# The late router gates as powers of e on GpSimd, one Gelu table load, and a new order in the last rounds of a decoder layer

## The reference, cut to what matters

```python
x = layernorm(x + linear_attention(x))              # softmax over q's head dim and over k's tokens
x = layernorm(x + cross_attention(x, ctx, ctx))     # 16 heads of 16
g = gelu(xt @ wg1 + bg1); logits = g @ wg2          # the router, 8 experts
probs = softmax(logits); top_vals, top_idx = top_k(probs, 2)
h = gelu(xt @ w_in[e]); o = h @ w_out[e]            # every expert, hidden size 512
y = sum over the two chosen experts of top_val * o
x = layernorm(x + y)
```

## Time and profile before

| | us |
|---|---|
| median of 3 executions | 430.15 |
| lowest, highest | 430.11, 433.90 |
| the profiled execution | 431.93 |
| its span, first to last instruction | 430.10 |

### The profile page before, as it was taken

How to read it: one execution, slowest core, us unless ns; L and a number is a source line. 1 busy time by engine, 2 the same in 40 slices (tenths; PEclk the granted TensorE clock), 3 DMA queues, 4 the chain that set the end, 5 groups by cost and what they waited for, 6 DMA issues and landing times. The chain is left out here.

```text
span 430.1 us, 12345 instructions
## 1 busy us (share of the span) xinstructions
PE 347.9 (81%) x4025; PEld 281.0 (65%) x4025; DVE 308.3 (72%) x912; ACT 222.1 (52%) x518; POOL 220.7 (51%) x287
## 2 busy tenths in 40 slices
PE   2977999999999999999887185759999999999200
PEld 1655777777777877777664053547899999988100
DVE  3767899888988889888777077468677666755193
ACT  3435676667666676766763045353544444444034
POOL 8335456676666766667258554643133333422273
PEclk9999999999999999999898588569999999999855
DMA  7520022220122211221012222325525322321393
GB/s 219 179 76 27 2 75 75 75 77 21 56 75 77 75 39 38 76 75 50 2 53 100 87 77 79 109 76 151 156 81 155 84 69 61 98 75 39 124 378 122
DMA packets 21387, 38.35 MB, mean 89 GB/s; under 512 B 3696, under 2 KB 11120, under 8 KB 21328
## 3 DMA queue, kind: packets, MB, share of 16 engines
q1 hardware_dynamic: 16768, 26.06, 19.8%
q0 software_dynamic: 3408, 9.41, 6.1%
q10 hardware_dynamic: 1152, 2.10, 1.3%
HBM read 24.71 MB, written 12.84 MB: 87 GB/s over the span
## 5 line engine op out<-in xcount | busy, mean ns | idle before, releaser
L575 POOL DMA_INDIRECT parts<-QKT,rows_all x39 | 37.8, 969 | 76.1 <-DVE QKT L1207 65.9
L328 PE MATMUL bank<-QS,EW 128*128 128x256 f16 (+1 forms) x384 | 62.6, 265 | 5.6 <-DVE XB L1021 5.6
L491 POOL TENSOR_TENSOR rstd<-veps,neghalf 128x1 f32<-128x1 f32 x48 | 39.6, 824 | 41.6 <-DVE veps L844 41.2
L1382 PE MATMUL bank<-EW,QV 128*128 x312 | 48.7, 273 | 1.8 <-DVE R L1199 0.8
L328 PE MATMUL bank<-XB,EW 128*128 128x256 f16 (+1 forms) x192 | 49.0, 264 | 0.0
L1199 DVE TENSOR_TENSOR R<-scratch,QV 128x512 f16<-128x512 f32 x39 | 26.7, 691 | 29.4 <-ACT scratch L764 17.9
L1126 DVE TENSOR_REDUCE NM<-bank 128x4 bf16<-128x512 f32 x64 | 39.6, 678 | 11.1 <-remote 10.1
L328 PEld LDWEIGHTS bank<-QS,EW 128*128 x384 | 37.7, 102 | 11.6 <-issue 6.1
L764 ACT ACTIVATE scratch<-bank 128x512 f32<-128x512 f32 x39 | 23.4, 600 | 40.5 <-PE bank L328 38.5
L506 POOL DMA_INDIRECT bkt<-REC,dest x32 | 32.9, 1029 | 21.3 <-issue 11.9
L699 ACT ACTIVATE rows_all<-bank 128x512 f32<-128x512 f32 x64 | 33.2, 603 | 18.2 <-remote 10.8
(11 more groups left out here) (240 smaller groups left out, 941.4 us busy)
## 6 DMA issues: line engine op xcount, KB each, us to landing
scratch<-w_in SPq DMA_DIRECT2D x8, 512.0 KB, 3.3
scratch<-w_out SPq DMA_DIRECT2D x8, 512.0 KB, 3.8
rows_all<-bkt SPq DMA_DIRECT2D x15, 262.0 KB
XC<-x SPq DMA_DIRECT2D x16, 128.0 KB, 3.3
XC<-ctx SPq DMA_DIRECT2D x16, 128.0 KB, 3.2
EW<-parts SPq DMA_DIRECT2D x8, 256.0 KB, 6.8
EW<-parts ACTq DMA_DIRECT2D x8, 256.0 KB, 7.4
out<-rows_all SPq DMA_DIRECT2D x8, 256.0 KB, 2.1
```

The costliest lines, as they stand in the source:

```text
L328: last = pe.matmul(dst, a(c), b(c), start=(c == 0 and i == 0), stop=(c == n - 1 and i == 2))
L491: pool.tensor_tensor(rstd[n][p][:], veps[n][p][:], neghalf[:, 0:1], ALU.pow).then_inc(s_rs[n], 1)
L575: pool.indirect_dma_start(parts, bass.IndirectOffsetOnAxis(ap=home[:, t, f:f + 1], axis=0), Y[t % 2][:, f, :], None).then_inc(s_put[t % 2] ...
L1382: last = pe.matmul(bank[4 + t % 2][:, f * D:(f + 1) * D], a[t % 2][:, h, f * P:(f + 1) * P], b[:, h, :], start=(h == 0 and i == 0 and f == 0),
```

## The change

Two things. The exponentials of groups 1 and 2 leave ScalarE: GpSimd computes them as powers of a constant tile `euler`, and ScalarE loads the Gelu table once, at a new step `hot:0` after the last reciprocal (group 0's exponentials stay on ScalarE). And the tails of GpSimd, VectorE and TensorE have a new order; on TensorE the up product of tile 0 is cut into two halves, `upa` and `upb`.

```diff
+        euler = sb("euler", [P, 1])
...
+            pool.memset(euler[:], float(np.exp(1.0))).then_inc(s_cst, 1)
...
+                if step == "exps":
+                    pool.wait_ge(s_off, b + 1)
+                    rows = slice(EDGE[b], EDGE[b + 1])
+                    n = EDGE[b + 1] - EDGE[b]
+                    pool.tensor_tensor(LE[:, rows, :].rearrange("p b e -> p (b e)"), euler[:].to_broadcast([P, n * NE]),
+                                       L[:, rows, :].rearrange("p b e -> p (b e)"), ALU.pow).then_inc(s_le, 1)
+                if step == "second":
+                    pool.wait_ge(s_gap, b + 1)
...
+                    pool.tensor_tensor(second[:, rows], euler[:].to_broadcast([P, EDGE[b + 1] - EDGE[b]]), gap[:, rows], ALU.pow)\
+                        .then_inc(s_second, 1)
...
-                     "lns:15 rec:15 X2T:13 gcp:13 gelu:1 X2T:14 exps:1 X2T:15 second:1 gcp:15 gelu:2 high:0 "
-                     "exps:2 second:2 high:1")
-            act.preload_act_table(ACT.Gelu)
+                     "lns:15 rec:15 hot:0 X2T:13 gcp:13 gelu:1 X2T:14 X2T:15 gcp:15 gelu:2 high:0 high:1")
...
-                     "x2T:13 cntpre:1 gh:13 ao2:15 x2T:14 lg:1 x2T:15 gh:15 cnt:1 lg:2 turn:0 cntpre:2 up:0 turn:1 cnt:2")
+                     "x2T:13 cntpre:1 gh:13 ao2:15 x2T:14 lg:1 x2T:15 gh:15 turn:0 cnt:1 cntpre:2 lg:2 upa:0 cnt:2 turn:1 upb:0")
```

More of the change, by code:

```diff
@@ L451, in _ @@
                 pool.memset(V2[p][:], 0.0).then_inc(s_cst, 1)
-            pool.wait_ge(s_cst, 11)
+            pool.wait_ge(s_cst, 12)
             for t in (ident, identb):
@@ L480, in _ @@
             pool.iota(spare_i[:], [[TW, MAXT], [P, HALVES]], base=0, channel_multiplier=1).then_inc(s_cst, 1)
-            pool.wait_ge(s_cst, 18)
+            pool.wait_ge(s_cst, 19)
             pool.affine_select(out=before[:], in_=before[:], compare_op=ALU.is_ge, fill=0.0, base=-1,
@@ L564, in _ @@
                      "pw0:14 qn:15 n1:14 x1b:14 n2:11 nr:12 pw0:15 "
[3 rows of a table removed]
+                     "pw1:15 sc:0 sc:1 sc:2 sc:3 x1b:15 sc:4 sc:5 pw2:12 sc:6 sc:7 sc:8 sc:9 sc:10 sc:11 pw2:13 sc:12 sc:13 sc:14 sc:15 sc:16 "
+                     "pw2:14 sc:17 sc:18 sc:19 pw2:15 "
+                     "exps:1 second:1 sc:20 sc:21 sc:22 sc:23 sc:24 sc:25 exps:2 second:2 sc:26 sc:27 sc:28 sc:29 sc:30 sc:31")
             def put(t):
@@ L710, in emit @@
                     gate_hidden(EDGE[b], EDGE[b + 1])
+                if step == "hot":
+                    act.preload_act_table(ACT.Gelu)
                 if step == "back":
@@ L1184, in _ @@
                      "QM1:14 R1:15 s1:15 "
[L1185 to L1188, removed]
+                     "mx0:14 n1:15 mx1:14 mx2:14 mx3:14 R2:12 s2:12 O2T:13 nr:13 QM1:15 full:0 n2:12 mx0:15 mx1:15 mx2:15 "
+                     "mx3:15 R2:13 s2:13 full:1 O2T:14 nr:14 full:2 n2:13 ewl:15 ewl:16 R2:14 s2:14 ewl:17 O2T:15 nr:15 R2:15 s2:15 n2:14 "
+                     "choice1:1 n2:15 choice2:1 gate1:1 dest:1 gate2:1 low:0 "
+                     "choice1:2 choice2:2 gate1:2 dest:2 gate2:2 whose:0 low:1 whose:1")
             def hidden_low(t):
@@ L1354, in expert_of, with up @@
                 return pe.value_load(texp[0:1, t:t + 1], min_val=0, max_val=NE - 1)
-            def up(t, e):
+            def up(t, e, hs=range(HC)):
                 pe.wait_ge(s_tTl, t + 1)
@@ L1364, in up @@
                 wi_h, wi_l = (EW_v[:, e, lo, 0, :].rearrange("p (k h) -> p k h", k=KC) for lo in range(2))
-                for h in range(HC):
+                for h in hs:
                     last = split3(pe, bank[2 * (t % 2) + h // hc][:, h % hc * n * P:(h % hc + 1) * n * P],
@@ L1368, in up @@
                                   lambda c: TXh[t % 2][:, c, 0:n * P], lambda c: TXl[t % 2][:, c, 0:n * P])
-                last.then_inc(s_up, 1)
+                if HC - 1 in hs:
+                    last.then_inc(s_up, 1)
             def down(t, e):
@@ L1637, in emit @@
                     tile_turn(b)
-                if step == "up":
+                if step == "upa":
                     pe.wait_ge(s_tables, 1)
@@ L1641, in emit @@
                     held[b] = expert_of(b)
-                    up(b, held[b])
+                    up(b, held[b], range(0, HC // 2))
+                if step == "upb":
+                    up(b, held[b], range(HC // 2, HC))
                 if step == "cntpre":
```

## The result

The changed kernel takes 441.58 us (median of 4 runs, 440.60 to 442.85), the kernel before, with one more execution than in the table above, 432.02 us: a ratio of 1.022, 95% interval 1.017 to 1.028. I had predicted 429.1 us and a range up to 434.8. The profiled execution has a span of 441.0 us where that of before had 430.1: 10.9 us more. That execution is the slowest of the four (442.85 us); the medians lie 9.6 us apart.

A forecast was written before the change was run, and what follows sets the result against it. Waits in 220 to 297 us, chiefly TensorE results held by scatters, set when the full expert stage starts. Terms -5.4 + 1.4 + 2.8 + 0.1 = -1.1 us on the median 430.15 gave 429.1 us; range 423.5 to 434.8.

The forecast's parts named there:

- term 1: Order of the rounds: earlier root and shorter scatter run release TensorE's results sooner, -5.4 us, between -10 and -0.5.
- The reading of the hold: Rounds 14 and 15: long unbroken scatter runs delay TensorE's results until about 1.8 us after the last scatter; guessed from two cases.
- hot:0, at nothing: ScalarE's early Gelu table load: puts X2T:13 back by a load, but lg:1 waits for x2T:14, so no cost.
- Term 2: Norm to second group's gates: +1.4 us for n2:14 behind round 15's statistics, +2.8 us with a 32-column power of 4.9 us.
- Rival C: Second group's exponentials on GpSimd: the wide power is cheap, about 1 us, giving 425.6 us; chance 0.16.
- D: Second group's gates: the power shuts out VectorE's two-operand instructions, 1.2 us more, giving 430.3 us; chance 0.08.
- Term 3: Second group's gates to up of tile 1: GpSimd's queue replaces the hold, 14.5 us against 14.4, +0.1 us.
- The last twelve scatters, at nothing: End of GpSimd's scatters: without a gap for gates they still end before the tables tile 3's load needs; no cost.
- Nothing changes after up:1: From up of tile 1 onward: TensorE sets the pace, so no further gain or loss.
- Rival A: Scatter run not broken at pw2:13, hold lasts to about 252 us: the order gains 0, total 434.5 us; chance 0.17.
- SP's queue keeps its order: SP's loads: their order in the queue is unchanged, listed among the things that cost nothing.
- both are through by then: TensorE before the second group's gates: cnt:1 now waits for turn:0, but both are finished in time; no cost.

The follow-up runs named there:

- late_sc: The kernel before with all 20 scatters of group 0 moved behind GpSimd's last root: 439.1 us in one run, where the kernel before takes 431.1.
- paused: The kernel before with GpSimd waiting at three places in its scatter run for results of TensorE, seven scatters standing later: 0.980 of the kernel before.
- no_hot: The changed kernel without the early Gelu table load, which ScalarE does at gelu:1 instead: 1.019 of the kernel before.
- before_again: The kernel before, unchanged, run again for its trace on a chip without the effect: 416.95 us.
- after_again: The changed kernel, unchanged, run again on a chip where the kernel before takes 415.9 us: 1.024 of it.
- p_order: order_only plus four GpSimd waits for TensorE's results, four group 0 scatters behind the last root: 1.023 of the kernel before, which took 416.0 us there.
- order_again: The order_only kernel, unchanged, run again on a chip where the kernel before takes 415.9 us: 1.007 of it.
- order_only: The changed kernel with groups 1 and 2's exponentials back on ScalarE and the old table loads, new order kept: 1.015 of the kernel before.

## Why the prediction was wrong

Predicted 429.1, measured 441.6, against a kernel before of 430.15 then and 432.02 beside the change. The step that failed is term 1: I took the held results as one hold that ends sooner, and priced it at -5.4 us; it was +2.0. No rival came near the measured time. Term by term, in the order of its steps, from the profiled executions of before and after:

- **The reading of the hold.** That TensorE's results are late beside scatters was right (late_sc, paused). Two things in it were wrong. "The first result that I see held ends 11 us into the run": after, round 13's sums end at about 227, 3.5 us into the run that starts at 223.59, and are seen at 230.94, in the middle of the run, so a hold needn't last until the run is over either. And it isn't one hold that is shorter or longer: the run of 15 became runs of 12, 5 and 3, and the first two each hold what falls due in them (no remote wait stands beside the last). I had counted only the first. The release comes 1.2 us (round 14), 0.4 us (round 15) and 1.2 us (up of tile 0) after the end of the last scatter, and not 1.8 us as in my two cases.
- **Term 1, -5.4 us (bounds -10 and -0.5).** It measured +2.0 at LS of round 15. At the scores of round 15 it was -4.2, close to what I took; I booked it there, and it was lost in the next run of scatters. "Some of it lost again behind scatters" was in the text, without a price. Behind the hold TensorE ran ao2:14 in 2.04 us and pv:15 in 3.6, where before they took 1.10 and 2.0: from 255 to 262 us the granted clock is 0.56, where before it was 1.00.
- **hot:0, at nothing.** Wrong, +1.5 us (no_hot). I looked at whether lg:1 waits for X2T:13, and not at what is queued behind gh:13 on TensorE: ao2:15, on round 15's own path, and at the clock that a wait leaves behind.
- **Term 2, +1.4 and +2.8 us.** Right in both mechanisms, a little small: 1.9 for n2:14 and 3.3 for the power, since 32 columns took 5.53 us and not 4.9 (0.16 us a column between 2.93 and 5.53 for 16 and 32, where the earlier trace rows give 0.14 from one to two). Rival C, the cheap power, is out. So is D: VectorE's products of two SBUF operands at 271.48 and 271.71, in the middle of the power that runs from 271.11 to 276.64, take 0.19 us each as ever. The rule of the Trainium skill (SBUF — State Buffer, "Who interferes with whom"), that the two shut each other out for the whole instruction, doesn't agree with this trace, now for a long one too.
- **Term 3, +0.1 us.** 14.5 us from gates to up of tile 1, as predicted, against 14.4 (8.8 - 8.7), and with the terms that I had summed: the six scatters end 8.2 us behind the gates, the power takes 2.93. It is right only on a chip with the effect. On the other, where nothing hid up of tile 0, it is 14.6 against 11.3: +3.3 us.
- **The last twelve scatters, at nothing.** Right. The last one starts 8.9 us later (296.96 against 288.11), but tile 3's load waits for the table `base` (SP, 3.6 us), as it did before (2.6 us).
- **"Nothing changes after up:1".** Wrong by 0.9 us up to tile 3 and 1.2 us behind it. From the start of up of tile 1 to its first Gelu it takes 5.99 us (292.75 to 298.74), before 5.06 (283.94 to 289.00): TensorE waited 6.71 us ahead of it, 4.43 before, and stays at the lower clock nearly to its end (0.62 from 298 to 299 us; before 0.77 already from 288 to 289). VectorE's table `base`, the load and the turn of tile 3 stand behind that Gelu and come later by as much. The 1.2 us behind tile 3 I have not taken apart.

The sum: 2.0 + 1.5 + 1.9 + 3.3 + 0.1 + 0.9 = 9.7 us at tile 3, and 10.9 at the end, against -1.1 forecast. Of these 12 us term 1 makes 7.4, hot:0 1.5, term 2 1.0, the stretch from up of tile 1 to tile 3 0.9 and the rest, whose cause stays open, 1.2. Rival A had the right sign and the wrong mechanism (the run was broken at pw2:13), and took term 1 at 0 as its worst.

On a chip without the effect the change costs as much, 1.024, with other terms. before_again against after_again: LS of round 15 +1.0, to veps +0.5, to L +1.9, to the gates +3.3, to up of tile 1 +3.3, 10.1 in all (270.59 and 280.66), 11.3 at the end. The order by itself costs little there (1.007); the powers make most of the rest, 3.3 + 3.3. The two kinds of chip agree in the loss, and that is chance: on the one a hold takes the order's gain back, on the other a load. There round 15's exponentials start 4.2 us sooner (238.67 against 242.90), nothing is held, and then ScalarE waits for the weights that its next step, ewh:17, reads:

```profile
247.56 1.06 ACT L756 ACTIVATE EW<-scratch 128x1024 f16<-128x1024 f32 x1 [6.55 <-DMA scratch<-w_out]
```

SP issues that load only when VectorE's ewl:15 has freed the buffer. In the old order ewl:15 stands ahead of round 14's output (O2T:14), in the new one behind it and behind n2:13, a move that the description of the change leaves out; so the load leaves at 242.76, against 241.49, though the rounds are ahead, and it takes 4.8 us to land, against 3.6. "SP's queue keeps its order" was right and not enough: its time hangs on VectorE's order. On the chip with the effect this wait doesn't show, since the rounds are late enough.

p_order was a lesson of the same kind: where I moved four scatters of group 0 behind the last root, tile 0's load came later, and in the new order turn:0 stands ahead of cnt:1 on TensorE. It waited 5.22 us for the load, and the gates of group 1 came at 267.80 where order_again had them at 262.60. My prediction had put that wait at nothing ("both are through by then") and set no condition on it.

## What to carry to other kernels

Moving a wide elementwise power to an idle GpSimd costs by the column, 5.5 us for 32, and counts in full when the result is on the path; ScalarE did it in 0.23, and I found no gain from the table loads saved. When a step moves, follow what is queued behind it on its own engine and behind each engine that waits for it. Where an engine's results arrive late beside another's burst, don't only reorder the burst: let it wait for exactly the results that are due, and measure on more than one chip before believing a gain or a loss of 3%.

## What was not expected of the hardware

- The same program takes 431 us on some chips and 416 us on others. Of the 14.9 us between the two profiled executions 13.4 are there by up of tile 1, in the stretch of GpSimd's indirect scatters: on the slower chips TensorE often goes on by only a few matmuls per scatter, and its results reach ScalarE and VectorE up to 11 us late (order_only, up of tile 0: ended at 280.48, seen at 291.50), in most cases until GpSimd pauses (1.8 us was enough). What in the chip does it stays open. In late_sc TensorE's few results beside 28 scatters in a row (up to 254 us, and after 25 us of waiting for a load at 280 us) were seen at once, so the density of TensorE's work may matter; that was seen once.
- A power on GpSimd over 1, 2, 4, 16 and 32 columns of 128 rows took 0.55, 0.69, 1.01, 2.93 and 5.53 us (one column with the exponent -0.5; two columns took the same with it and as a power of e).
